# A windowed-attention block with a 3x3 convolution: pads and normalised halo patches written by GpSimd instead of DVE

## The reference

```
v   = group_norm(x)                       # 32 groups of 2 channels, over 2 x 128 x 128, eps 1e-5
qkv = 1x1 conv (64 -> 192) + bias, then depthwise 3x3 conv, zero padding 1, + bias
windows of 8 x 8, 4 heads of 16 channels:
  attn = softmax(q k^T * temperature)     # channel by channel, 16 x 16, over the 64 pixels
  out  = attn v
  gate = gelu(v w_mlp^T + b_mlp)          # over the 64 pixels of a window
out = 1x1 conv (64 -> 64) of (out * gate) + bias
result = x + out
```

## Time and profile before

| what | value |
|---|---|
| median of three runs | 827.38 us (827.29 to 830.31) |
| profiled execution | 824.44 us |
| its span | 822.7 us |
| PE busy | 718.9 us (87%) |
| DVE busy | 615.0 us (75%) |
| ACT busy | 506.1 us (62%) |
| POOL busy | 0.3 us |
| mean granted PE clock | 0.992 of full speed |

### The profile page before, as it was taken

One profiled execution on the slowest core, in us unless ns is written; L12 is line 12 of the kernel. 1 busy time (PEld: TensorE's weight loads), 2 busy tenths in 40 slices (PEclk: granted clock), 3 DMA queues, 4 the chain that ended last, 5 costly groups with the idle time before them and its releaser, 6 DMA issues.

```text
span 822.7 us, 29929 instructions
## 1 busy us (share of the span) xinstructions
PE 718.9 (87%) x13704; PEld 620.3 (75%) x13704; DVE 615.0 (75%) x1021; ACT 506.1 (62%) x628; POOL 0.3 (0%) x5
## 2 busy tenths in 40 slices
PE   3968898989988898999989898999989898989965
PEld 3956777777877777887868787887878777877854
DVE  2715497989897886878777886868777787868676
ACT  2553465767566565767576575766566665758554
POOL 0000000000000000000000000000000000000000
PEclk9999999999999999999999999999999999999997
DMA  9723131533334040405023040403022140412022
GB/s 235 266 102 110 18 110 54 177 88 131 112 100 141 5 159 3 158 3 171 5 67 111 17 162 4 161 3 139 25 73 92 40 123 2 159 18 104 3 65 40
DMA packets 26461, 73.13 MB, mean 89 GB/s; under 512 B 9464, under 2 KB 15992, under 8 KB 21272
## 3 DMA queue, kind: packets, MB, share of 16 engines
q1 hardware_dynamic: 26076, 69.31, 26.6%
q10 hardware_dynamic: 258, 1.90, 1.2%
HBM read 54.43 MB, written 16.78 MB: 87 GB/s over the span
## 4 chain that ended last, share of the span: by engine, by line
PE 77%; DVE 11%; issue 5%; ACT 5%; DMA 1%; DVEq 0%; ACTq 0%
PE work L600 24%; PE work L580 18%; PE turn_ps L666 8%; PE gate_ps L645 8%; PE score_ps L679 7%; PE work L551 5%; DVE z L343 4%; PE turn_ps L654 4%; PE score_ps L636 3%; ACT v_t L297 2%; ACT z L275 2%; DMA z<-in_hot 1%; DVE scores L462 1%; DVE total L458 1%; ACT scores L291 1%
## 5 line engine op out<-in xcount | busy, mean ns | idle before, releaser
L580 PE MATMUL work<-consts,patches 64*100 64x192 f32 x2048 | 203.8, 337 | 14.3 <-DVE patches L407 6.5
L600 PE MATMUL work<-z,dw 109*64 109x64 f32 x6144 | 199.6, 223 | 13.2 <-DVE z L343 12.3
L600 PEld LDWEIGHTS work<-z,dw 109*64 109x64 f32 x6144 | 187.3, 138 | 22.0 <-issue 14.6
L580 PEld LDWEIGHTS work<-consts,patches 64*100 64x100 f32 x2048 | 156.0, 164 | 39.3 <-issue 11.4
L275 ACT ACTIVATE z<-work 100x768 f32<-100x768 f32 x158 | 121.5, 809 | 86.1 <-PE work L580 86.1
L275 ACT ACTIVATE qkv<-work 128x1024 f32<-128x1024 f32 x63 | 64.5, 1024 | 128.4 <-PE work L600 128.4
L343 DVE COPY z<-work 100x768 f32<-100x768 f32 x98 | 91.2, 954 | 33.4 <-PE work L580 32.6
L666 PE MATMUL turn_ps<-v_t,probs_t 64*64 64x64 f32 x2048 | 74.2, 222 | 30.9 <-ACT v_t L297 20.6
L666 PEld LDWEIGHTS turn_ps<-v_t,probs_t 64*64 64x64 f32 x2048 | 65.5, 136 | 46.3 <-ACT v_t L297 29.4
L645 PE MATMUL gate_ps<-consts,qkv 128*128 128x128 f32 x512 | 74.6, 289 | 24.7 <-issue 23.3
L343 DVE COPY qkv<-work 128x1024 f32<-128x1024 f32 x33 | 40.4, 1225 | 73.3 <-PE work L600 73.3
(11 more groups left out here) (45 smaller groups left out, 640.2 us busy)
## 6 DMA issues: line engine op xcount, KB each, us to landing
staged<-in_x SPq DMA_DIRECT2D x18, 1024.0 KB, 5.0
out_y<-staged SPq DMA_DIRECT2D x15, 1024.0 KB, 5.2
T<-in_x SPq DMA_DIRECT2D x12, 1152.0 KB, 8.8
seen<-in_x SPq DMA_DIRECT2D x16, 512.0 KB, 3.8
qkv<-in_x SPq DMA_DIRECT2D x6, 1024.0 KB, 24.9
T<-in_x SPq DMA_DIRECT2D x3, 1088.0 KB, 9.3
z<-in_edges SPq DMA_DIRECT2D x5, 288.0 KB
out_y<-staged SPq DMA_DIRECT2D x4, 256.0 KB, 3.8
```

Of the source, the lines that this page charges most:

```text
L580: last = nc.tensor.matmul(to[0:NPATCH, t, b * QKV:(b + 1) * QKV], patches[image, b, g], w1[image], start=True, stop=True)
L600: last = nc.tensor.matmul(to[h * HW:(h + 1) * HW, m // 8, m % 8 * NW:(m % 8 + 1) * NW], dw[0:K, c, :], z[0:K, c, :], start=True, stop=True)
```

## The change

`pad` and `normalise` are taken from DVE's list and put into GpSimd's, which now loops over all 16 chunks by itself. A semaphore `norm_ready`, raised by the last instruction of `normaliser`, tells GpSimd that mean and inverse deviation of a pair are there; a semaphore `pad_chain` stands for the waits between pads. The instructions, their operands and their other waits are the same.

```
@@ gpsimd
+            def link(ins):
+                links[0] += 1
+                ins.then_inc(pad_chain, 1)
+                pool.wait_ge(pad_chain, links[0])
+
+            def pad(edge, pair):
...
+                link(nc.gpsimd.tensor_scalar(edge, over, norm[:, pair, 0:1], None, ALU.add))
+
+            def normalise(n):
+                pair, band = n // BANDS, n % BANDS
+                pool.wait_ge(norm_ready, pair + 1)
+                if n:
+                    pool.wait_ge(t_in, n * 16)
+                else:
+                    pool.wait_ge(zeroed, 1)
+                    pool.wait_ge(first_copied, 1)
...
+                if n:
+                    wait_full(pool, ("mix", n - 1, COLS - 1))
+                for b in range(2):
...
+                    last = nc.gpsimd.tensor_scalar(patches[:, b].rearrange("p w (r c) -> p w r c", r=PATCH), windows,
+                                                   norm[:, pair, 0:1], norm[:, pair, 1:2], ALU.subtract, ALU.mult)
+                last.then_inc(patches_ready, 1)
+
             nc.gpsimd.memset(zeros[:], 0.0).then_inc(zeroed, 1)
+            pool.wait_ge(zeroed, 1)
+            for n in range(CHUNKS):
+                normalise(n)
@@ vector
-                link(nc.vector.tensor_tensor(norm[:, pair, 1:2], small[:, 4:5], small[:, 5:6], ALU.mult))
+                nc.vector.tensor_tensor(norm[:, pair, 1:2], small[:, 4:5], small[:, 5:6],
+                                        ALU.mult).then_inc(norm_ready, 1)
...
-            normalise(0)
             for g in range(1, COLS, 2):
                 evacuate_mix(dve, copy, 0, g)
-            normalise(1)
...
-                if a == 3 and n + 1 < CHUNKS:
-                    normalise(n + 1)
```

More of the change, by code:

```diff
@@ L131, in build @@
         chain = sem("chain")
+        pad_chain = sem("pad_chain")
+        norm_ready = sem("norm_ready")
         first_copied = sem("first_copied")
@@ L264, in _ @@
         def _(pool):
+            links = [0]
+            def link(ins):
[3 more added lines that the diff above has]
+            def pad(edge, pair):
+                size = edge.shape[1] * edge.shape[2]
+                over = zeros[:, 0:size] if size <= 2 * (BAND + 2) else zeros[:, 0:1].to_broadcast([P, size])
+                over = over.rearrange("p (r c) -> p r c", r=edge.shape[1])
+                link(nc.gpsimd.tensor_scalar(edge, over, norm[:, pair, 0:1], None, ALU.add))
[7 more added lines that the diff above has]
+                    pool.wait_ge(first_copied, 1)
+                if band == 0:
+                    pad(T[:, :, 0:W + 2:W + 1], pair)
+                    pad(T[:, 0:1, :], pair)
+                if band == BANDS - 1:
+                    pad(T[:, BAND + 1:, :], pair)
+                if n:
+                    wait_full(pool, ("mix", n - 1, COLS - 1))
+                for b in range(2):
+                    rows = T[:, b * WS:b * WS + PATCH, :]
+                    line = rows.ap[1][0]
+                    windows = bass.AP(rows.tensor, rows.offset, [rows.ap[0], [WS, COLS], [line, PATCH], [1, PATCH]])
+                    last = nc.gpsimd.tensor_scalar(patches[:, b].rearrange("p w (r c) -> p w r c", r=PATCH), windows,
+                                                   norm[:, pair, 0:1], norm[:, pair, 1:2], ALU.subtract, ALU.mult)
+                last.then_inc(patches_ready, 1)
             nc.gpsimd.memset(zeros[:], 0.0).then_inc(zeroed, 1)
+            pool.wait_ge(zeroed, 1)
+            for n in range(CHUNKS):
+                normalise(n)
         @block.scalar
```

## The result

The changed kernel takes 899.11 us (median of four runs, 890.25 to 901.10) against 827.34 us: ratio 1.0851, 95% interval 1.0814 to 1.0887. That is 71.8 us slower, where 6.5 us were forecast. Lines of `patches`, L407 before, are L301 now; L444 and L462 are L459 and L477; the PE's L580, L600, L645 and L666 are L591, L611, L656 and L677.

The account below looks back on a forecast made before the run. TensorE was taken as the bound, freed DVE time counting only where TensorE waits for DVE. Start 3.7, change of pair 0.8 and meeting 2.0 made +6.5 us: 834 us for the median, range 826 to 856.

Parts of the forecast that it names:

- the start: Before the first channel mix: pads and two patch instructions on GpSimd take longer than on DVE, +3.7 us.
- the change of pair: Chunk 8: the evacuation, gates and scores start 1.7 us earlier, but the mix waits for patches; +0.8 us.
- D: Price of one patch instruction of 1600 columns on GpSimd: estimated at 2.7 us, with ends 1.1 and 5.4.
- the meeting: GpSimd reading SBUF during DVE's softmax, in nine chunks: bounded between nothing and 7.2 us, taken as 2 us.
- the removals: Normalisations taken off DVE: 14 of 16 worth nothing, since DVE there waits for TensorE anyway.
- Rival 4: DVE is the bound after all, and its 14 chunk-end passes come off the path: 802 us; chance 0.03.
- the high end: Upper price of a GpSimd patch instruction: a read, two arithmetic operations and a write, 5.4 us.
- Rival 3: Long patch on GpSimd, 5.4 us, from strided rows of 10 columns: 843 us without a meeting; chance 0.10.
- D outside 1.4 to 3.5 us: Sign that the prediction is wrong: GpSimd's mean patch instruction time falls outside these limits.
- rival 2: DVE's L444 and L462 stand still for GpSimd's reads in nine chunks: 7.2 us, 839 in all; chance 0.14.
- the far end: Patch of 5.4 us that also meets the softmax: 64 us more, about 907; left out of the range.
- no late patches in the chunks: All other chunks: T loads go out as before and GpSimd finishes before the mix; zero cost.

Follow-up runs that it names:

- experiment 3: Kernel before, with DVE's patch instructions of chunks 1 to 15 left out (those of chunk 0 used again): 824.75 us against 828.42, ratio 0.9956.
- experiment 6: Kernel of experiment 5, with GpSimd's patch instructions waiting for the probabilities of steps a = 2 and a = 3: 828.43 us, ratio 1.0016.
- experiment 4: Kernel before, with nine GpSimd instructions (a memset, then forms of the patch instruction) added in its first 54 us: one run, 832.63 us.
- the halves: Changed kernel, with each GpSimd patch instruction cut into two of 800 columns: 845.51 us, ratio 1.0221.
- experiment 5: Changed kernel, with the normalisations of chunks 0 and 8 back on DVE and GpSimd doing the other 14: 882.96 us, ratio 1.0685.
- experiment 1: Kernel before, with GpSimd also doing the patches of 14 chunks, which DVE then does again: 897.03 us; without chunk 1, 886.10 us.
- experiment 2: Kernel before, with GpSimd adding eight memsets of 1600 columns per chunk, writing SBUF without reading it: 836.41 us; without chunk 1, 826.82 us.

## Why the prediction was wrong

Of the three terms of the sum, the start (+3.7) and the change of pair (+0.8) were too small because of D, and the meeting (+2.0) was far too small; the clock was not in the sum at all.

**Right: what the removals are worth.** Fourteen of sixteen were called worth nothing, and the change of pair 1.7 us of earlier evacuation. Experiments 3 and 6 bear this out, and chunk 6's period fell by 1.7 us in the changed kernel too. That DVE's busy time would fall by 35.6 us did not come: the holds made it rise by 22.4. Rival 4 (802 us) is refuted: 33 us less on DVE gave 3.7.

**Wrong: the price D.** The prediction took D = 2.7 us, "since a copy-like instruction must at least read and write". The memset rows it rested on price a pass at 0.83 ns a column, and a copy does go at 0.95. But the count of passes was wrong: a copy, which reads and writes, takes 1.52 us and so one such pass (1.4 us by the rows), not two, and arithmetic is not free beside it, with 2.8 us for the first operation and 1.4 for the second. That the high end, four equal passes or 5.4 us, lies only 7% under the measured 5.77 is in part luck, since it has the read and the write 1.2 us too high and the first operation 1.5 us too low. The mistake was to take the middle of three candidates where nothing in the trace spoke for it. Rival 3 gave the long price another reason, the rows of 10 columns; experiment 4 shows that they cost nothing (5.76 us against 5.74). With D measured, the start is 10.96 us against +3.7 forecast, of which 0.85 lie ahead of `norm`: the prediction's own sum gives 9.8 with D = 5.77. The change of pair is about 9 us (the halves, which have no meetings left in it, show 10.9 in chunk 7 less 1.7 in chunk 6) against +0.8. By the prediction's own sum the halves' patches (12.14 us) make up 7.6 of these 9.2; behind the PE's wait of 9.53 us the clock was 0.50 to 0.65, and the first 32 mix matmuls took 4.68 us in place of 3.41. The best case of a tight loop from the Trainium skill (GPSIMD Engine Reference, section 3.1), 1.8 cycles an element, is far from reached by this instruction: 3.4 ns a column would be 4.1 cycles at the 1.2 GHz that the page gives (an estimate). Section 4.1 of that page calls one-input operations roughly line-rate. The copy comes near that (1.52 us, where DVE takes 1.107 for the same columns with arithmetic), the instruction with scalars does not (5.77). The prediction named D outside 1.4 to 3.5 us as a sign that it is wrong, and that sign came.

**Wrong: the meeting, by far the largest.** It was priced at 2 us in all, and is 52 to 56 (experiment 5). The mechanism was named as rival 2, with its place and the slack of 1.3 us; the sum for D = 5.4 with a meeting was 907 and stood in rival 3 as the far end. The measured 899 is near it, and the two were given 0.24 together, with a range that ended at 856. The nearness is in part luck: 907 had 15 us for start and change of pair, where 20 were found, and 64 for the meetings, as one stall until both GpSimd instructions end and without the clock. Three things were mis-set. First, 2 us was chosen on the ground that GpSimd's first instruction would be over a tenth of a microsecond before the shift began; a number that hangs on D should have been worked out at both ends of D, and at D = 5.8 GpSimd's 11.5 us cross the shift and the scaling of every such step. Second, the price was taken for one stall, but each of the nine steps has two: in chunk 8 1.30 and 3.41 us, less slack, 2.87 of waiting on the PE. Third, nothing stood in the sum for the clock, to which 19.0 us of the 75.5 go over the whole run (the PE's longer busy time, the change of pair included): 1.4 us more for the next depthwise unit behind a wait of 3.56 us, in that chunk a third of the loss (2.87 + 1.36 + 0.15 for the scores = 4.38 of the 4.37 by which that chunk is longer).

The Trainium skill (SBUF — State Buffer, section "Who interferes with whom") states this rule, that two SBUF inputs on DVE and a GpSimd instruction that reads SBUF exclude each other and that one that only writes does not. Experiments 1 and 2 agree on both counts. The section "Summary: rules for kernel authors" of the same page says that the second to issue is blocked until the first finishes. The measurements differ, and they decide: the hold ended after 4.16 us of 5.77, and after 0.87 of 3.04. A rule of a page that speaks against a change and that no row contradicts deserved more than 0.14.

**Right: no late patches in the chunks.** T's loads kept their place, and the PE waited for patches only twice, at the start and at chunk 8, as stated.

## What to carry to other kernels

Work moved to an idle engine is worth only what the loaded engine's path gets back: read, for each place, what that engine does right behind the work; if it waits for another engine there, the move gives nothing. GpSimd may copy at about 1 ns a column but needs 2.7 ns with one and 3.6 ns with two scalar operations (1600 columns), and while it reads it stops DVE instructions with two SBUF operands; place it between them (a wait on a semaphore is enough) or cut it into shorter instructions, and never put it where the next engine waits. When an unknown price enters a sum twice, work the whole sum out at both of its ends before choosing.

## What the runs showed of the hardware that was not expected

The hold is not in proportion to the instruction: 0.53, 0.87 and 4.16 us from GpSimd's start for 400, 800 and 1600 columns of the same operation, and 1.4 us for a copy of 1600 (GpSimd from 536.57, a shift of 1.26 us at 537.41). Cutting one instruction in two therefore took away more than half of the stall. The hold works both ways: GpSimd's own instruction took 6.29 us in place of 5.77 where a scaling was already running when it began (scaling from 132.13 to 132.83, GpSimd from 132.19), which costs it no more than what is left of a 0.69 us instruction. And the PE's waits for the transpose in nine chunks (3.4 to 6.1 us each) and for the patches at the change of pair (8.9) each come with a stretch at the lower clock, enough to bring the mean granted clock from 0.992 to 0.959, with 19 us more of busy time for the same matmuls.
